# A selective-scan block: part of the state products moves from VectorE to ScalarE and GpSimd, and dt gets one buffer

## The reference

```python
dA = jnp.exp(dt[..., None] * A)
dBu = dt[..., None] * Bm[:, :, None, :] * u[..., None]
def step(h, inp):
    dA_t, dBu_t, C_t = inp
    h = dA_t * h + dBu_t
    y_t = jnp.einsum('bdn,bn->bd', h, C_t)
    return (h, y_t)
y = ys.swapaxes(0, 1) + u * Dskip
y = y * jax.nn.silu(z)
return y @ W_out.T
```

## Time and profile before

| | us |
|---|---|
| median of 3 runs | 3207.58 |
| lowest and highest run | 3205.63, 3210.02 |
| the profiled execution | 3209.26 |
| its span, first to last instruction | 3207.4 |
| mean granted TensorE clock, share of full | 0.887 |

### The profile page before, as it was taken

How to read it: one execution, slowest core, us unless ns; L and a number is a source line. 1 busy time by engine, 2 the same in 40 slices (tenths; PEclk the granted TensorE clock), 3 DMA queues, 4 the chain that set the end, 5 groups by cost and what they waited for, 6 DMA issues and landing times.

```text
span 3207.4 us, 41798 instructions
## 1 busy us (share of the span) xinstructions
PE 2488.6 (78%) x12320; PEld 1435.1 (45%) x12320; DVE 2755.0 (86%) x3590; ACT 1748.9 (55%) x3158; POOL 1774.5 (55%) x1497
## 2 busy tenths in 40 slices
PE   3578888988988357788878777778787777788787
PEld 1233434434433145554555444545545445455453
DVE  6565776776775499999999999999999999999993
ACT  2334676575676555555555555555555555555552
POOL 1111222222221177777777777787777877777773
PEclk8789999999988677998889889899898988898989
DMA  6543322323332442122122121221221221212101
GB/s 216 206 156 130 127 93 100 126 100 107 111 116 77 148 175 70 47 80 70 56 85 72 42 75 62 75 71 59 81 71 54 72 73 54 70 60 79 43 27 40
DMA packets 152830, 286.68 MB, mean 89 GB/s; under 512 B 40128, under 2 KB 89536, under 8 KB 148224
## 3 DMA queue, kind: packets, MB, share of 16 engines
q1 hardware_dynamic: 152576, 283.71, 26.0%
HBM read 174.09 MB, written 109.58 MB: 88 GB/s over the span
## 4 chain that ended last, share of the span: by engine, by line
POOL 26%; issue 21%; DVE 16%; PE 1%; POOLq 1%; ACT 0%; DMA 0%; DVEq 0%; SPq 0%
POOL dbu L1009 19%; DVE h L1177 9%; DVE y L1187 5%; POOL x L1033 2%; POOL o L1039 1%; POOL y L1029 1%; POOL dbu L1014 1%; POOL carry L1020 1%; PE p_g L1312 1%; POOLq L40 1%; DVE tokt L1209 1%; PE p_g L1302 0%; POOL small L69 0%; DVE q L1200 0%; DVE x L1220 0%
## 5 line engine op out<-in xcount | busy, mean ns | idle before, releaser
L1096 ACT ACTIVATE p_da<-dt,neg_a 128x255 f32<-128x255 f32 x2048 | 891.5, 468 | 870.0 <-DVE h L1177 869.7
L1177 DVE TENSOR_TENSOR_SCAN h<-p_da,dbu 128x512 f32<-128x512 f32 x1024 | 1192.8, 1207 | 19.7 <-POOL dbu L1014 15.5
L1009 POOL TENSOR_TENSOR dbu<-dtu,bb 128x1024 f32<-128x1024 f32 x512 | 1197.1, 2360 | 0.8 <-issue 0.2
L1279 PE MATMUL p_ht<-ident,h 128*128 128x128 f32 x4096 | 644.3, 318 | 340.9 <-DVE h L1177 338.4
L1279 PEld LDWEIGHTS p_ht<-ident,h 128*128 128x128 f32 x4096 | 561.1, 165 | 449.8 <-issue 266.1
L1187 DVE SCALAR_TENSOR_TENSOR y<-p_ht,ct,y 128x1024 f32<-128x1024 f32 x512 | 646.6, 1263 | 0.0
L1312 PE MATMUL p_g<-wo,tokt 128*128 128x512 f16 x1536 | 362.4, 395 | 3.3 <-DVE tokt L1209 3.3
L1321 PE MATMUL p_g<-wz,xz 128*128 128x512 f16 x1536 | 351.2, 386 | 0.0
L706 PE MATMUL p_u<-xz,wu 128*128 128x512 f16 x1536 | 350.3, 385 | 0.0
L358 POOL TENSOR_TENSOR late<-dt,u 128x512 f32<-128x512 f32 x64 | 82.4, 1287 | 425.4 <-DVE dt L550 425.4
L697 PE MATMUL p_ffn<-tern,xt 128*128 128x512 f16 x1024 | 258.2, 416 | 63.0 <-DVE xt L500 62.9
(11 more groups left out here) (112 smaller groups left out, 2754.3 us busy)
## 6 DMA issues: line engine op xcount, KB each, us to landing
bb<-b_scratch SPq DMA_DIRECT2D x128, 256.0 KB, 3.3
xin<-in_x SPq DMA_DIRECT2D x32, 512.0 KB, 4.4
x_scratch<-x SPq DMA_DIRECT2D x32, 512.0 KB, 3.3
xz_scratch<-xz SPq DMA_DIRECT2D x16, 1024.0 KB, 5.5
y_scratch<-late SPq DMA_DIRECT2D x32, 512.0 KB, 2.9
dt_scratch<-dt SPq DMA_DIRECT2D x64, 256.0 KB, 2.2
dtu_scratch<-late SPq DMA_DIRECT2D x64, 256.0 KB, 2.5
dt<-dt_scratch SPq DMA_DIRECT2D x16, 1024.0 KB, 6.4
```

Source lines behind the costliest of these rows:

```text
L1009: nc.gpsimd.tensor_tensor(state[:, 4 * f:4 * f + 4, :], dtu[par][:, 4 * f:4 * f + 4, :], bb[n // NB % 2][:, n % NB:n % NB + 1, :].to_broad ...
L1096: ins_ = nc.scalar.activation(p_da[p % 2][:, k * T2 + 1:(k + 1) * T2], dt[par][:, g, 1:], ACT.Exp, scale=neg_a[:, g, n:n + 1])
L1177: nc.vector.tensor_tensor_scan(h[n % 2][:, 2 * p:2 * p + 2, :].rearrange("p g t -> p (g t)"), p_da[p % 2][:], dbu[n % 2][:, 2 * p:2 * p + ...
L1279: mm = nc.tensor.transpose(p_ht[t][:, g * P:(g + 1) * P], h[n % 2][:, g, t * P:(t + 1) * P], ident[:])
```

## The change

In the second pass, for the second token half (t=1) and the six states 4, 6, 7, 8, 10 and 13 (table PARTED), DVE's accumulation is left out. Instead ACT multiplies the PSUM tile by C of the state on its way to SBUF (part_state, called in slot n for state n-1 behind the decays of pairs 2 and 3): for state 4 into the new tile y2, for the others into the new tile part. POOL adds part to y2 (add_part, in the slots of table PART_ADDED, behind times_b), and in slot 1 of the next chunk adds y2 to y (merge). ACT counts y_added[1] up in DVE's place. There is one buffer part, so ACT's next evacuation waits for POOL's addition before. Gate for t=1 waits for the merge.

dt gets one buffer of 8 groups in place of two. Each pair of groups is loaded by a DMA of its own in SP's slot 15, when the decays of state 15 of that pair are done, and has a semaphore of its own. This frees the room for y2 and part.

```diff
--- before.py
+++ after.py
@@ -790,7 +790,7 @@
         carry = sb("carry", [P, NS, G])
         edge_dt = sb("edge_dt", [P, 1, G])
         factor = [sb(f"carry_factor{i}", [P, NS, G]) for i in range(2)]
-        dt = [sb(f"dt_{i}", [P, G, T2]) for i in range(2)]
+        dt = sb("dt_", [P, G, T2])
         dtu = [sb(f"dtu_{i}", [P, G, T2]) for i in range(2)]
         ct = [sb(f"ct_{i}", [P, TT2, NS]) for i in range(2)]
         NB = 2
@@ -804,6 +804,8 @@
         tokt = sb("tokt", [P, 2, G, P], F16)
         xn = sb("xn_2", [P, D])
         o = [sb(f"o{i}", [P, HALF]) for i in range(2)]
+        y2 = sb("y2", [P, D])
+        part = sb("y2_part", [P, D])
         small = sb("small2", [P, 48])
         stats, mv, vn, sn = small[:, 0:12], small[:, 12:14], small[:, 14:16], small[:, 16:18]
         gs = [small[:, 20 + 8 * t:28 + 8 * t] for t in range(TT2)]
@@ -820,7 +822,9 @@
         carry_set, da_zeroed, product_done = sem("carry_set"), sem("da_zeroed"), sem("product_done")
         edge_loaded, edge_arg, edge_done = sem("edge_loaded"), sem("edge_arg"), sem("edge_done")
         bias_loaded = sem("bias2_loaded")
-        dt_loaded = [sem(f"dt2_loaded{i}") for i in range(2)]
+        dt_loaded = [sem(f"dt2_pair_loaded{p}") for p in range(G // 2)]
+        dtu_loaded = [sem(f"dtu2_loaded{i}") for i in range(2)]
+        part_added = sem("y2_part_added")
         y_loaded = [sem(f"y2_loaded{i}") for i in range(2)]
         b_loaded = [sem(f"b2_loaded{i}") for i in range(2)]
         xz_loaded = sem("xz2_loaded")
@@ -845,6 +849,9 @@
                14: [("f", 0, 1)], 15: [("n", 1, 0), ("n", 1, 1)]}
         ZED = {2: [("z", 0, 0)], 3: [("z", 0, 1)], 11: [("z", 1, 0)], 12: [("z", 1, 1)]}
 
+        PARTED = (4, 6, 7, 8, 10, 13)
+        PART_ADDED = {8: 6, 9: 7, 10: 8, 12: 10, 14: 13}
+
         def flags(i):
 
             if isinstance(i, int):
@@ -893,12 +900,18 @@
                 def load_scan(c, par):
 
                     wait_alone(sp, y_added[1], (c - 1) * NS)
-                    for name, tile in (("dt", dt), ("dtu", dtu)):
-                        sp.dma_start(tile[par][:], dram[name][bass.ds(c, 1)].rearrange("c p g t -> p (c g) t")
-                                     ).then_inc(dt_loaded[par], 16)
+                    sp.dma_start(dtu[par][:], dram["dtu"][bass.ds(c, 1)].rearrange("c p g t -> p (c g) t")
+                                 ).then_inc(dtu_loaded[par], 16)
                     with nc.allow_non_contiguous_dma(reason="64 bytes a token"):
                         sp.dma_start(ct[par][:], dram["ct"][bass.ds(c * T2, T2), :].rearrange("(t p) n -> p t n", p=P)
-                                     ).then_inc(dt_loaded[par], 16)
+                                     ).then_inc(dtu_loaded[par], 16)
+
+                def load_dt(c, p):
+
+                    if not (isinstance(c, int) and c == 0):
+                        wait_alone(sp, da_done, (c - 1) * (NS * 4) + (NS - 1) * 4 + p + 1)
+                    sp.dma_start(dt[:, 2 * p:2 * p + 2, :], dram["dt"][bass.ds(c, 1), :, 2 * p:2 * p + 2].rearrange(
+                        "c p g t -> p (c g) t")).then_inc(dt_loaded[p], 16)
 
                 def load_y(c, par):
                     if not (isinstance(c, int) and c < 2):
@@ -943,6 +956,8 @@
                 def prologue():
                     with nc.allow_non_contiguous_dma(reason="constants"):
                         sp.dma_start(neg_a[:], ins["A_log"].rearrange("(g p) n -> p g n", p=P)).then_inc(const_loaded, 16)
+                    for p in range(G // 2):
+                        load_dt(0, p)
                     load_scan(0, 0)
                     load_b(0, 0)
                     load_edge(1)
@@ -972,6 +987,9 @@
                             store(i - 2, *{1: (0, 1), 6: (1, 0), 7: (1, 1)}[n])
                         if c_on and n in (1, 7):
                             load_x1(i - 1, n // 7)
+                        if z_on and more(i) and n == 15:
+                            for p in range(G // 2):
+                                load_dt(i + 1, p)
                         if c_on and n == 15:
                             store(i - 1, 0, 0)
                         if z_on and more(i) and n == 9:
@@ -999,7 +1017,7 @@
 
                 def times_b(i, par, n):
                     if n == 0:
-                        wait(pool, dt_loaded[par], (i - par) * 24 + 48)
+                        wait(pool, dtu_loaded[par], (i - par) * 16 + 32)
                     if n % NB == 0:
                         wait(pool, b_loaded[n // NB % 2], (i * (NS // NB // 2) + n // NB // 2 + 1) * 16)
                     state = dbu[n % 2]
@@ -1020,8 +1038,20 @@
                     nc.gpsimd.tensor_tensor(carry[:, n, :], h[n % 2][:, :, T2 - 1], factor[1 - cpar][:, n, :],
                                             ALU.mult).then_inc(carry_done, 1)
 
+                def add_part(c, k):
+                    wait(pool, y_added[1], c * NS + PARTED[k] + 1)
+                    wait(pool, part_added, c * len(PARTED) + k - 1)
+                    nc.gpsimd.tensor_tensor(y2[:], y2[:], part[:], ALU.add).then_inc(part_added, 1)
+
+                def merge(c, cpar):
+                    wait(pool, y_added[1], c * NS + NS)
+                    wait(pool, part_added, c * len(PARTED) + len(PARTED) - 1)
+                    nc.gpsimd.tensor_tensor(y[cpar][1][:], y[cpar][1][:], y2[:], ALU.add).then_inc(part_added, 1)
+
                 def gate(c, cpar, t):
                     wait(pool, y_added[t], c * NS + NS)
+                    if t:
+                        wait(pool, part_added, (c + 1) * len(PARTED))
                     for x in range(2):
                         b, m = place(c, "z", t, x)
                         wait(pool, g_free[b], m + 1)
@@ -1049,6 +1079,8 @@
                             times_b(i, par, n)
                             if edge(i) and n == 8:
                                 edge_argument(i + 2, par)
+                            if n in PART_ADDED:
+                                add_part(i, PARTED.index(PART_ADDED[n]))
                         if e_on:
                             if n == 1:
                                 finish(i - 1, i - 2, 0, 1)
@@ -1057,6 +1089,8 @@
                             if n in (6, 7):
                                 finish(i, i - 2, 1, n - 6)
                         if c_on:
+                            if n == 1:
+                                merge(i - 1, 1 - par)
                             if n in (2, 3):
                                 gate(i - 1, 1 - par, n - 2)
                             if n in (10, 13):
@@ -1087,15 +1121,26 @@
                     nc.scalar.activation(factor[par][:], factor[par][:], ACT.Exp).then_inc(edge_done, 1)
 
                 def decays(i, par, n, pairs):
-                    if n == 0 and pairs[0] == 0:
-                        wait(act, dt_loaded[par], (i - par) * 24 + 48)
                     for p in pairs:
+                        if n == 0:
+                            wait(act, dt_loaded[p], i * 16 + 16)
                         wait(act, scan_done, i * (NS * 4) + n * 4 + p - 1)
                         for k in range(2):
                             g = 2 * p + k
-                            ins_ = nc.scalar.activation(p_da[p % 2][:, k * T2 + 1:(k + 1) * T2], dt[par][:, g, 1:], ACT.Exp,
+                            ins_ = nc.scalar.activation(p_da[p % 2][:, k * T2 + 1:(k + 1) * T2], dt[:, g, 1:], ACT.Exp,
                                                         scale=neg_a[:, g, n:n + 1])
                         ins_.then_inc(da_done, 1)
+
+                def part_state(i, par, n):
+                    k = PARTED.index(n)
+                    if n == PARTED[0]:
+                        wait(act, dtu_loaded[par], (i - par) * 16 + 32)
+                        wait(act, part_added, i * len(PARTED))
+                    else:
+                        wait(act, part_added, i * len(PARTED) + k - 1)
+                    wait(act, ht_full[1], i * NS + n + 1)
+                    nc.scalar.activation((part if k else y2)[:], p_ht[1][:], ACT.Copy, scale=ct[par][:, 1, n:n + 1]
+                                         ).then_inc(y_added[1], 1)
 
                 def tanh(i, t, x):
                     b, m = place(i, "z", t, x)
@@ -1143,6 +1188,8 @@
                             tanh(i, n // 12, n - 3 if n < 12 else n - 12)
                         if z_on:
                             decays(i, par, n, (2, 3))
+                            if n - 1 in PARTED:
+                                part_state(i, par, n - 1)
                             if edge(i) and n == 10:
                                 edge_decays(i, par, 2)
                             if isinstance(i, int) and i == 0 and n == 0:
@@ -1179,6 +1226,8 @@
                                                      0.0, ALU.mult, ALU.add).then_inc(scan_done, 1)
 
                 def add_state(c, par, n, t):
+                    if t and n in PARTED:
```

(1 more changed line is left out.)

## The result

The changed kernel took **3230.03 us** (median of 4 runs, 3226.42 to 3233.21). The kernel before took 3207.75 us beside it (4 runs, 3205.63 to 3210.02). The ratio is 1.0069 with a 95% interval of 1.0052 to 1.0086: it is slower by 22 us. The forecast was 3224 us within 3207 to 3243. The profiled execution took 3231.22 us, with a span of 3229.4 us against 3207.4 before.

What follows compares the result with a forecast made beforehand. The prediction took DVE to set the pace of the second pass. Its terms, -112.3 + 100.2 + 13.1 + 12 + 3 = +16 us, gave 3224 us, within 3207 to 3243.

Steps and rivals of the forecast that it cites:

- removed accumulations: Second pass: six second-half accumulations per chunk leave DVE, 96 at 1.17 us, -112.3 us.
- fifth addition: State 13, evacuated and added in slot 14 ahead of dbu(15): DVE waits 6.26 us in 16 chunks, +100.2 us.
- merge: Merge on POOL in slot 1, ahead of keep(0) and dbu(2): DVE waits 0.87 us in 15 chunks, +13.1 us.
- waits for PE: DVE waits for PE's transposes of states 5 and 9: 0.4 + 0.4 us a chunk in 15 chunks, +12 us.
- start of the pass: Second pass's start: three more DMAs issued ahead of those POOL waits for, +1.3 us.
- end of the pass: Second pass's end: the merge goes ahead of both gates, 0 to 1.17 + 2.30, middle +1.7 us.
- The chain from S(14) to S(15): From DVE's first scan in slot 14 to that in slot 15, through evacuation, addition, keep and dbu(15): 11.93 us.
- The four hidden additions: POOL's additions for states 6, 7, 8 and 10, one slot behind their evacuation: cost nothing, 0.7 us left.
- dt in one buffer: 0: Chunk's end: reloading dt by pairs into a single buffer is covered by 3.8 us, so costs 0.
- Rival (1): The saving stands because POOL's last addition does not hold dbu(15): sum -84, 3123 us; chance 0.09.
- Rival (2): No change to measure, as PE's transposes turn out in time: sum +4, 3212 us; chance 0.17.
- Rival (4): Semaphore waits add 0.3 us at three late POOL places per chunk: about +14, 3238; part of the slower case.

Runs made afterwards that it cites:

- e1: The changed kernel with only POOL's addition of state 13 moved from slot 14 to slot 15, behind keep and product: 3138.07 us.
- e2: The changed kernel with state 12 parted in place of state 13, its addition still in slot 14: 3129.52 us.
- e4: e1 with POOL's merge moved from slot 1 to slot 2, behind the gate of the first half: 3118.29 us.
- e3: The changed kernel without evacuations, additions or merge, all accumulations back on DVE; only dt in one buffer stays: 3214.58 us against 3209.39 before the change.
- e9: The changed kernel with states 2, 4, 6, 7, 8, 10, 12 parted, merge behind the gate in slot 2, first loads reordered: 3102.07 us.

## Why the prediction was right

**The terms.** The idle intervals alone don't add up to the time: when a record follows its predecessor at once they overlap, and after each wait this overlap of about 0.09 us (1.26 against 1.17) is lost too. With it the sum closes:

| term of the prediction | predicted | measured in the two profiles |
|---|---|---|
| removed accumulations | -112.3 | 96 fewer at 1.17 = -112.3 |
| fifth addition | +100.2 | 98.8 idle + 16 x 0.09 = 100.3 |
| merge | +13.1 | 13.2 idle + 15 x 0.09 = 14.5 |
| waits for PE | +12 | 6.7 idle + 15 x 0.09 = 8.0 |
| start of the pass | +1.3 | 17.83 - 15.68 = +2.15 |
| end of the pass, to DVE's last instruction | +1.7 | 51.48 - 50.51 = +0.97 |
| the last product and what follows it | none | 11.84 - 13.46 = -1.62 |
| first chunk, POOL | not seen | 2.6 + 3 x 0.09 = 2.9 |
| loop turns (3.3 idle), ACT's q, smaller | not seen | about +4.5 |
| before the second pass | none | +2.3, nothing was changed there |

From the first scan to the last accumulation that is -112.3 + 100.3 + 14.5 + 8.0 + 2.9 + 4.5 = 17.9 us; the profiles have 2037.3 against 2019.1, +18.2. With the edges the span grew by 22.0 us (3229.4 - 3207.4), and the sum had said 16. That the two totals lie so close is in part luck: the terms that were not seen (+2.9, +4.5 and +2.3) came to 9.7 us, and the PE term, 4 us too large, and the last product, 1.6 us shorter, took part of it back.

**Point by point.** The chain from S(14) to S(15) was put at 11.93 us and measured 11.98: the evacuation at S + 3.18 was exact, its record 1.10 instead of the bound of 1.13, POOL's start 0.15 behind it instead of 0.09, and the addition 2.32 from start to start instead of 2.30. e1 and e2 show that it is this chain and not POOL's load. The 0.87 us before state 2 was right for the size and the cause (e4). The four hidden additions are hidden, with one exception that I didn't follow: I took a chunk from the middle, and **the first chunk** differs. Its slots 8 to 11 have none of the small pieces that stretch DVE's slots, so DVE would ask every 5.67 us where a state is parted, and POOL with an addition in each of three slots needs 7.37. POOL's timeline shows two of them, from keep to keep:

```profile
1182.28 0.20 POOL L1038 TENSOR_TENSOR carry<-h,carry_factor 128x8 f32<-128x8 f32 x1
...
1187.34 2.36 POOL L1044 TENSOR_TENSOR y<-y,y_part 128x1024 f32<-128x1024 f32 x1
1189.66 0.21 POOL L1038 TENSOR_TENSOR carry<-h,carry_factor 128x8 f32<-128x8 f32 x1
...
1197.03 0.21 POOL L1038 TENSOR_TENSOR carry<-h,carry_factor 128x8 f32<-128x8 f32 x1
```

DVE then waits 0.56, 1.62 and 0.44 us.

**What was off in size.** The PE term (0.4 + 0.4 us a chunk) was too large: of the 30 places that it counts DVE waited in 13, 6 before the accumulation of state 5 and 7 before that of state 9, for 0.47 us on average. It lay inside the bounds of 0 to 1.6. "dt in one buffer: 0" was right for the reload and wrong for the whole: e3 costs 5.2 us; its profile has 2.5 at the start, which I had put at 1.3 and was 2.15 in the change, and 4.0 at the loop turns, where I had not looked. The end of the pass cost 1.0 on DVE's side where I had charged 1.7: DVE's reduction there waits 4.90 us for POOL instead of 1.42, but the transposed tokens behind it wait 1.70 instead of 3.42, and the next wait for PE 7.62 instead of 8.42. Behind DVE's last instruction 1.6 us came back on PE's clock. The last 32 matmuls, before and after:

```profile
3194.12 8.75 PE L1302 MATMUL p_g<-tern,tokt 128*128 128x512 f16 x32 [1.51 <-DVE tokt L1209]
```

```profile
3217.74 7.07 PE L1351 MATMUL p_g<-tern,tokt 128*128 128x512 f16 x32 [1.51 <-DVE tokt L1258]
```

The granted clock was 0.83 from 3193 to 3203 us before, and 1.00 from 3217 to 3225 us after. The forecasts for busy time, "about 120 us less" on DVE and 108 more on ACT, took whole records: DVE's fell by 107.8, which is 96 x 1.17 less the overlap lost at the waits. The 96 evacuations of 1.09 are 105 us as records, but ACT rose by 94.3: from start to start one takes 0.99 (2121.29 to 2122.28 in the chunk above).

**The rivals.** Rival (1), that the saving stands, fell for the reason given, the order on POOL and ACT; e1 with 3138 and e2 with 3130 are near the 3123 that it would have been. But the prediction says there that the order of POOL and ACT leaves no other place for that addition, and this was wrong: in e1 it stands one slot later and DVE never waits for it. Rival (2) had the wait for PE smaller than I took, which was true, but too little to decide. Rival (4), an added latency at each of POOL's late places, would have shown in the chain from S(14) to S(15), which was longer by 0.05 us and not by 0.3; POOL's start behind the evacuation took 0.06 more than assumed.

The Trainium skill, Perfetto Trace Analysis, "Identifying the Most-Contended Engine", says to improve the engine with the highest occupancy first. DVE is that one here, 86% of the span, and what left it was what the rule asks for. Taken alone it gave 3095 us. The change measured 3230, and e9, with 16 more accumulations off DVE but each addition placed where POOL and ACT have room, 3102. So the rule found the engine and said nothing of the price.

## What to carry to other kernels

When work moves from the bounding engine to one that runs in order and feeds it, follow that queue slot by slot: what stands behind the moved instruction, and when the thing it waits for is ready. The slack of an engine at 55% is no price; here one addition in one slot cost 100 us of 112, and a slot later DVE waited for it nowhere. A producer and its consumer on another queue should stand in different slots. Check the first and last turn of a loop by themselves, since the pieces that give the others their slack may be missing there.

## What I had not expected of the hardware

At the five places where the loop turns, ACT's first decays in e3 began after 2.75 to 3.90 us of idle time that the profile puts down to nothing but issue, and DVE lost 0.58 to 0.91 us at each. In the kernel before ACT waited there for DVE's scan (1.02 to 1.22 us) and DVE lost nothing. The changed kernel has a wait in the same five places, 0.24 to 0.84 us, which its profile puts down to POOL's carry or to issue:

```profile
2139.03 2.34 DVE L1224 TENSOR_TENSOR_SCAN h<-p_da,dbu 128x512 f32<-128x512 f32 x2 [0.82 <-POOL carry L1038]
```

POOL's carry and ACT's decays had both ended by then (2138.24 and 2138.07 us), so neither is plainly the cause. It is 3.3 us of idle in this run and 4.0 in e3. What the kernels have in common there is a burst of packets on the instruction queues, and what the kernel before lacks is the loads of dt at the same moment (the queues under e3). Whether the one delays the other was not tried and stays open.
